# The order and spacing of the q.k rows in a chunked delta-rule attention beside a ternary feed-forward net

## The reference, cut to what matters

```
x = x + 0.5 * ffn(layernorm(x))                 # four layers of ternary weights
x = x + attention(layernorm(x))
x = x + 0.5 * ffn(layernorm(x))

# attention: q, k, v, beta from one projection, 16 heads of 16; k is normalized; then over all tokens
retrieval = einsum('bhij,bhj->bhi', S, k_t)
S = S + einsum('bhi,bhj->bhij', beta_t * (v_t - retrieval), k_t)
o_t = einsum('bhij,bhj->bhi', S, q_t)
# and x + scan_out @ w_out + b_out;   x is (4, 1024, 256) in float32
```

## Time and profile before

| | us |
|---|---|
| median of 3 runs | 1806.7 |
| lowest, highest | 1805.43, 1808.03 |
| the profiled execution: time | 1805.1 |
| the profiled execution: span | 1803.4 |
| PE busy in it | 1724.1 |
| DVE busy | 1241.3 |
| POOL busy | 1208.7 |
| ACT busy | 1055.8 |

### The profile page before, as it was taken

One profiled execution on the slowest core, in us unless ns is written; L12 is line 12 of the kernel. 1 busy time (PEld: TensorE's weight loads), 2 busy tenths in 40 slices (PEclk: granted clock), 3 DMA queues, 4 the chain that ended last, 5 costly groups with the idle time before them and its releaser, 6 DMA issues.

```text
span 1803.4 us, 29772 instructions
## 1 busy us (share of the span) xinstructions
PE 1724.1 (96%) x10030; PEld 1069.7 (59%) x10030; DVE 1241.3 (69%) x2890; ACT 1055.8 (59%) x2115; POOL 1208.7 (67%) x1501
## 2 busy tenths in 40 slices
PE   6989989999999999999999999999999999999999
PEld 5865545555555555555555555588655555555588
DVE  5255777777776877868767687777776868767331
ACT  4656555565656565656556474666656555655454
POOL 4463876667676667677676767677776767675653
PEclk9999999999999999999999999999999999999999
DMA  7100000000000000000000000000000000000000
GB/s 286 49 1 1 1 1 1 1 1 1 1 1 1 24 1 24 1 1 1 1 1 1 1 24 1 1 25 1 1 1 1 1 1 13 1 1 13 1 13 13
DMA packets 5270, 23.16 MB, mean 13 GB/s; under 512 B 640, under 2 KB 1664, under 8 KB 3584
## 3 DMA queue, kind: packets, MB, share of 16 engines
q1 hardware_dynamic: 5120, 21.26, 3.2%
HBM read 17.06 MB, written 4.19 MB: 12 GB/s over the span
## 4 chain that ended last, share of the span: by engine, by line
PE 63%; POOL 10%; issue 10%; DVE 8%; ACT 7%; POOLq 0%; ACTq 0%; DVEq 0%
PE ffn_bank L1101 38%; PE ffn_bank L1084 6%; PE att_bank L1150 5%; PE att_bank L1122 4%; POOL hid_lo L584 4%; PE state_bank L1158 2%; POOL pairs_lo L621 2%; POOL pairs L613 2%; PE att_bank L1137 2%; ACT hid L700 2%; PE att_bank L1138 2%; PE att_bank L1042 2%; ACT L700 1%; DVE hid L841 1%; ACT hid_hi L676 1%
## 5 line engine op out<-in xcount | busy, mean ns | idle before, releaser
L1101 PE MATMUL ffn_bank<-hid_hi,w_sb 128*128 128x512 f16 (+1 forms) x2736 | 904.8, 346 | 8.6 <-ACT gate L687 4.6
L1101 PE MATMUL ffn_bank<-hid_lo,w_sb 128*128 128x512 f16 (+1 forms) x2736 | 904.6, 346 | 0.0
L584 POOL TENSOR_TENSOR hid_lo<-hid,hid_hi 128x512 f16<-128x512 f32 (+1 forms) x456 | 462.8, 1030 | 289.9 <-ACT hid_hi L676 289.6
L613 POOL TENSOR_TENSOR pairs<-KQ 128x32 f32<-128x32 f32 (+15 forms) x496 | 325.9, 667 | 122.8 <-DVE KQ L868 104.6
L1101 PEld LDWEIGHTS ffn_bank<-hid_hi,w_sb 128*128 128x128 fp8e4 x2736 | 275.7, 101 | 206.9 <-issue 11.7
L1101 PEld LDWEIGHTS ffn_bank<-hid_lo,w_sb 128*128 128x128 fp8e4 x2736 | 268.4, 98 | 205.4 <-issue 12.1
L621 POOL TENSOR_TENSOR pairs_lo<-pairs,pairs_hi 128x448 f16<-128x448 f32 (+15 forms) x416 | 313.2, 758 | 72.4 <-ACT pairs_hi L748 72.1
L748 ACT CAST pairs_hi<-pairs 128x448 f16<-128x448 f32 (+15 forms) x416 | 174.9, 438 | 159.7 <-POOL pairs L613 154.4
L676 ACT CAST hid_hi<-hid 128x512 f16<-128x512 f32 (+1 forms) x456 | 234.9, 552 | 31.0 <-DVE hid L841 30.4
L700 ACT ACTIVATE hid<-ffn_bank,par_sb 128x512 f32<-128x512 f32 (+1 forms) x304 | 171.6, 616 | 120.7 <-PE ffn_bank L1101 119.9
L1084 PE MATMUL ffn_bank<-xn_hi,w_sb 128*128 128x512 f16 (+1 forms) x532 | 177.4, 348 | 11.5 <-DVE hid L841 8.3
(11 more groups left out here) (92 smaller groups left out, 2134.5 us busy)
## 6 DMA issues: line engine op xcount, KB each, us to landing
NK<-in_w SPq DMA_DIRECT2D x11, 1024.0 KB, 6.0
X<-in_x SPq DMA_DIRECT2D x7, 512.0 KB, 3.4
out<-X SPq DMA_DIRECT2D x7, 512.0 KB, 2.6
wqkvb_sb<-in_wqkvb SPq DMA_DIRECT2D x1, 1024.0 KB, 9.1
X<-in_x SPq DMA_DIRECT2D x2, 256.0 KB, 6.6
out<-X SPq DMA_DIRECT2D x2, 256.0 KB, 2.1
wout_sb<-in_wout SPq DMA_DIRECT2D x1, 256.0 KB, 10.0
par_sb<-in_par SPq DMA_DIRECT2D x1, 24.0 KB, 2.4
```

What stands on the lines that cost most here:

```text
L584: pool.tensor_tensor(hid_lo[layer % 2][:, m, call.cols], hid[:, u % HID_BUFFERS, call.cols], hid_hi[layer % 2][:, m, call.cols], ALU.subtr ...
L613: pool.tensor_tensor(packed(pair(pairs, q, dot), n), later, earlier, ALU.mult).then_inc(pairs_made if dot in SPLIT else pairs_ready, 1)
L1101: mm = nc.tensor.matmul(ffn_ps(call, j), weight(name, kk, 2 * pair + i), v[:, kk, cols], start=kk == 0 and part == 0, stop=kk == KT_FF - 1 ...
```

## The change: q.k rows from the widest to the narrowest, with other distances

The table of ticks for the q.k rows is replaced, and row t is looked up by `QK_AT`, so that tick `E_QK[0]` belongs to row 15 and the last to row 0. Two conditions that named the first and the last row now name them by the new order.

```diff
-E_QK = [1, 4, 6, 7, 12, 14, 16, 19, 21, 23, 28, 32, 34, 36, 39, 41]
+E_QK = [2, 5, 8, 11, 14, 17, 20, 23, 25, 28, 30, 32, 34, 36, 38, 41]
+QK_ROWS = list(range(C - 1, -1, -1))
+QK_AT = dict(zip(QK_ROWS, E_QK))
...
-    return found + [("qk", f - 1, t) for t in range(C) if E_QK[t] == e and 1 <= f <= PARTS]
+    return found + [("qk", f - 1, t) for t in range(C) if QK_AT[t] == e and 1 <= f <= PARTS]
...
-                    act.wait_ge(pairs_made, SPLIT["qk", w - HALVES, C - 1] + 1)
+                    act.wait_ge(pairs_made, SPLIT["qk", w - HALVES, QK_ROWS[-1]] + 1)
...
-                if t == 0:
+                if t == QK_ROWS[0]:
```

## The result

| | before | after |
|---|---|---|
| median of 19 runs each, us | 1805.98 | 1809.19 |
| ratio, 95% interval | | 1.0017 (1.001 to 1.0023) |
| span of the profiled execution | 1803.4 | 1807.6 |
| time of the profiled execution | 1805.1 | 1809.36 |

What follows compares the result with a forecast made beforehand. PE was taken as the bound, busy 1724.1 of 1803.4 us. Terms +3.3 + 2.4 + 0.5 - 3.4 - 1.0 = +1.8 gave 1806.9, or 1808.5 beside the median of 1806.7; range 1799 to 1821.

Steps and rivals of the forecast that it cites:

- The forecast case: Whole kernel: costs on POOL and DVE early outweigh late gains, +1.8 us, 1808.5 us; chance 0.50.
- its own signs: Profile after: q.k low-half waits at widths 416 to 480 move to ticks 2 to 12, 2 to 6 us in all.
- the rival of the early room: Before tick 12: POOL works ahead, nothing is lost early, late gains of -4.4 us stay, 1802.3; chance 0.18.
- POOL early: Five ticks before the frame to tick 12: 4.85 us more POOL work per frame overflows in three frames, costing 3.3 us.
- overflow = cost: POOL's work beyond the early window counted as lost time: 0.6, 1.6 and 1.1 us in frames 5, 12 and 15.
- Late q.k waits: POOL loses 4.2 us in ticks 24 to 34, so PE's waits at widths 416 to 480 go: gain 3.4 us.
- DVE early: To tick 12: wide rows put 3.1 us more on DVE ahead of the first `turn_u`; cost 2.4 us.
- Second update: The second `turn_u`, tick 34, has 0.75 us more DVE work ahead, largely absorbed by the wait behind: cost 0.5 us.
- DVE's end: Ticks 38 to 42: 2.5 us of DVE's work go, PE waits less for `mix` and `ffn_out`: gain 1.0 us.
- The port: Norm of tick 37: narrow POOL rows beside it save DVE up to 0.7 us in such a frame; counted as nothing.
- The rival in which POOL becomes the bound: POOL's backlog from ticks -5 to 24 carries on, q.k pays what k.k pays: about +14 us, 1820.6; chance 0.19.
- The one in which the late stretch loosens: Late ticks: layer norm comes forward, half of PE's `xn`, `Uz`, `hid` waits go: -14 us, 1792.5; chance 0.07.

Runs made afterwards that it cites:

- double low halves: POOL computes each q.k low half twice, once into an unread buffer: the kernel before 1905.16 us, the changed kernel 1855.79 us.
- light early rows: Changed kernel, DVE taking one column per run for the four widest q.k rows (ticks 3 to 12) only: 1802.36 us.
- light middle rows: Changed kernel, DVE taking one column per run for the five q.k rows of width 256 to 128 only: 1805.14 us.
- all rows light: Changed kernel, DVE taking one column per run for every q.k row, whatever its width: 1797.18 us.
- the order alone: Kernel before with q.k rows widest first, but at the old ticks: 1812.27 us, ratio 1.0035.

## Why the prediction was right, and which terms were not

The forecast case came about: 1808.5 predicted, 1809.19 measured. Half of its mechanism, waits moved from POOL's late low halves to DVE's early queue, is in the traces and in the runs. The other half, a price paid on POOL early, is not. The sum, +1.8 us on the profiled execution, was 2.5 short of the measured +4.3, and that it came this close is in part luck: its largest term, +3.3, measured 0, and without it the sum would have been -1.5, a gain. What filled its place are the middle ticks, the gain of 1.0 that did not come, and 2 us of late starts without a term. Another 0.7 us of the closeness came from the median of three runs that it stands on, 1806.7, where 19 runs gave 1805.98. By its own signs, q.k waits of 0 to 1 us in all spoke for the rival of the early room, and "issue" and `X`, which it did not name, grew by 1.3 and 0.7 us.

*POOL early, +3.3 predicted: 0.* POOL did fill up as predicted. These are the windows of ticks -5 to 12 in frames 5, 8, 12, 13 and 15 of the changed kernel, columns and frames as in the earlier trace rows:

```profile
605.10:624.20 19.10, 18.21 (x101) 10.16 (x100) 17.06 (x45) 11.28 (x23) 18.32 (x20) 1.00 0.02 6
906.10:924.00 17.90, 17.90 (x102) 10.33 (x101) 13.19 (x37) 10.68 (x23) 15.25 (x17) 1.00 0.00 0
1306.90:1325.00 18.10, 17.26 (x98) 10.00 (x98) 15.18 (x41) 9.38 (x19) 18.10 (x20) 1.00 0.00 1
1404.90:1423.70 18.80, 17.72 (x100) 10.17 (x100) 16.52 (x42) 11.83 (x23) 14.45 (x16) 1.00 0.00 1
1603.60:1621.50 17.90, 17.90 (x101) 10.34 (x101) 13.26 (x38) 8.94 (x19) 17.55 (x20) 1.00 0.00 1
```

Frame 8's POOL, 15.25, is what the sum had (15.3), and in frames 12 and 15 POOL is busy 18.10 of 18.10 and 17.55 of 17.90 us. Yet no wide row waits. The step that failed here is "overflow = cost": I had taken the window's end as the time at which all the work in it is due. A full window only means that POOL has stopped running ahead. What it had in hand covers it, as I read it; the run with double low halves shows that the cover ends, with 19.3 us of waits in ticks 0 to 16. That POOL no longer runs ahead shows in its groups: the 18.1 us that it idled before products, waiting for a pair buffer that PE still had to read, are gone. The group of before:

```profile
L613 POOL TENSOR_TENSOR pairs<-KQ 128x32 f32<-128x32 f32 (+15 forms) x496 | 325.9, 667 | 122.8 <-DVE KQ L868 104.6 <-PE att_bank L1140 18.1
```

and the one of after:

```profile
L615 POOL TENSOR_TENSOR pairs<-KQ 128x256 f32<-128x256 f32 (+15 forms) x496 | 326.2, 667 | 105.8 <-DVE KQ L870 105.8
```

The rival in which the early room takes it all was right about this one term. (Its number was 1802.3; the 1804.1 written beside it is the forecast's 1808.5 less the same 4.4.)

*Late q.k waits, -3.4 predicted: -3.4.* 4.3 us of waits under `head_ones` became 0.9. The run with double low halves shows the mechanism much larger.

*DVE early, +2.4 predicted: +2.7 in idle time.* Most of it fell in frames 6, 13 and 14, and less in 5 than its full window suggests: frame 5 had 17.06 us of DVE in 19.10 and waited 0.9 us in all (0.6 for `hid`, 0.3 for `Uz`) in that window. Frame 14, which I hadn't counted, starts a feed-forward call whose first `X` sat behind the rows of 512 and 480. At `Uz` of tick 15 only frames 5 and 6 wait, and not 13, where `hid` does. The mixed waits at `hid`, `X` and `Uz` are one cause, as the run with light early rows shows by removing them all.

*Second update, +0.5 predicted: +2.3, with all that went on in ticks 24 to 42.* This is the term that was mis-sized. I priced only the 0.75 us by which `turn_u` of tick 34 gets more ahead of it, and let the waits behind it absorb the most of it. In the trace the waits for `Uz` at tick 35 grew by 1.1 us, PE waited 1.3 us more on "issue", and `xn` fell by only 0.3 us. The run with light middle rows shows that DVE's q.k work there costs 3.4 us of time; how much of that the change brought is not shown by it, since no such cut was made in the kernel before.

*DVE's end, -1.0 predicted: nothing found.* The changed kernel's windows of ticks 12, 24, 38 and 43 in frame 8, beside the earlier trace rows:

```profile
924.00:936.70 12.70, 12.70 (x75) 7.76 (x74) 7.30 (x17) 4.42 (x11) 11.53 (x16) 1.00 0.00 1
936.70:951.10 14.40, 12.98 (x72) 6.75 (x71) 13.40 (x33) 10.50 (x21) 6.12 (x12) 1.00 0.01 2
951.10:957.70 6.60, 5.73 (x30) 3.11 (x29) 6.07 (x14) 4.34 (x10) 2.53 (x3) 1.00 0.00 0
```

DVE was still busy 6.07 of 6.60 us, 1.2 less than before and not 2.5, since other work moved in. I found no wait that the kernel before had there and the changed one has not. POOL, with 6.12 of 14.40 us in place of 9.98 of 14.90, is where the relief lies, and it is worth only the 3.4.

*The port.* The norm of tick 37 in frame 5 on DVE's timeline, after, where the earlier trace rows had 1.37:

```profile
649.99 0.72 DVE L830 TENSOR_TENSOR xn<-xc,roots 128x512 f32<-128x512 f32 x1
```

and POOL's timeline beside it, where the earlier trace rows had 1.60:

```profile
650.12 0.69 POOL L623 TENSOR_TENSOR pairs_lo<-pairs,pairs_hi 128x32 f16<-128x32 f32 x1
```

Here the norm, which started first, ran at its short time, and POOL's 32-wide row took 0.69 us against a mean of 0.25. That fits the rule quoted from the Trainium skill ("SBUF — State Buffer", "Who interferes with whom"). The prediction put the wrong partner beside the long norm of before, though. That one started at 648.96, when POOL was in the feed-forward's `hid_lo`; row 512 began at 649.74 only, later than a norm of 0.68 us would have ended:

```profile
648.62 1.15 POOL L584 TENSOR_TENSOR hid_lo<-hid,hid_hi 128x512 f16<-128x512 f32 x1
```

So narrow rows there are not shown to save DVE anything. The shorter norm gained nothing in the kernel's time that I can see, since PE does not wait there.

The rest, about 2 us of the 4.3, is the late starts named with the result; the sum had no term for them. The rival in which POOL becomes the bound fell with the waits at zero. The one in which the late stretch loosens fell too: `xn`, `Uz` and `hid` together wait longer than before. For `hid` and `Uz` DVE holds the stretch, as the light middle rows show. What holds `xn` is not shown: in ticks 24 to 42 its waits are 4.7 us in the changed kernel and don't fall with DVE's q.k work made light (6.0 with all rows light, 5.5 with the middle ones) nor change much with POOL's low halves doubled (4.9).

## What to carry to other kernels

When a row of work passes through several engines, ask for each of them where its widest pieces meet its busiest stretch: the order that unloads one (POOL late, 3.4 us here) loads another (DVE; 2.7 us of idle time early and up to 2.3 in the middle). Making one engine's cost flat shows in two runs which engine pays, and a cut in only one stretch shows where. A window that is full of work is not yet a wait; a producer with buffers in hand has first to lose its lead. An order and the spacing made for it are one change: here each alone was twice as bad as both. And a sum can come out near with its largest term at nothing, so check the terms, and not the total.

## What the hardware showed that I had not expected

*After a wait of PE the granted clock can fall for 3.4 us at a time.* In the kernel before, windows of PE around its first long wait and after it (the columns as in the earlier trace rows):

```profile
99.00:103.00 4.00, 0.98 (x8) 0.75 (x9) 0.41 (x2) 2.92 (x5) 3.91 (x5) 1.00 0.00 0
103.20:106.60 3.40, 3.40 (x17) 2.17 (x15) 0.51 (x2) 1.85 (x6) 3.40 (x5) 0.50 0.00 0
```

In the changed kernel, the same places and one later:

```profile
99.00:103.00 4.00, 0.91 (x8) 0.42 (x7) 0.60 (x1) 2.34 (x5) 3.33 (x4) 1.00 0.00 0
103.20:106.60 3.40, 3.40 (x28) 2.65 (x26) 1.84 (x3) 3.39 (x10) 3.40 (x5) 1.00 0.00 0
...
121.20:124.60 3.40, 3.40 (x19) 2.40 (x17) 2.38 (x4) 3.06 (x7) 3.40 (x5) 0.51 0.00 0
```

At a granted clock of 0.50 (1.2 of 2.4 GHz) 17 matmuls fit where 28 fit at full clock. The stretch came at 103.2 in one trace and not in the other after almost the same idle time, so a wait may or may not cost its clock too. A stretch of 3.4 us at 0.50 does the work of 1.7 us at full clock, so each costs some 1.7 us (an estimate). Ahead of the last matmuls the kernel before had three such stretches and the changed one two, of which one each, at 263.6 and 264.6 us, in frames 0 to 16; the run with the order alone had seven, one of them in frame 8. The wait ahead of it on PE's timeline:

```profile
950.99 0.29 PE L1160 MATMUL state_bank<-Uz,Kz 128*128 128x64 f32 x1 [1.53 <-DVE Uz L949]
```

and the window 1.4 us later:

```profile
952.40:955.80 3.40, 3.40 (x9) 1.22 (x8) 3.33 (x9) 0.24 (x1) 0.76 (x1) 0.50 0.00 0
```

Such stretches are part of what the longer waits cost beyond their idle time; they don't explain the change itself, which had one fewer.

*One execution ran 3.5 times as long.* Of the run with four narrow rows in front, one execution took 6401.56 us, with its matmuls started some 0.84 us apart in place of 0.216, at a granted clock that the records give as 1.0. Nothing else in the runs repeats it, and its cause is open.
